# Feed-forward stages software-pipelined over batches, their square roots computed as powers on GpSimd

## The reference, cut to what matters

```python
def _ternary_linear(x, w):
    alpha = jnp.mean(jnp.abs(w))
    w_t = jnp.sign(w) * (jnp.abs(w) > 0.5 * alpha)          # weights -1, 0, 1
    rms = jnp.sqrt(jnp.sum(x * x, axis=-1, keepdims=True)) / jnp.sqrt(d)
    return jnp.einsum('bsd,fd->bsf', x / (rms + EPS), w_t)
h = gelu(_ternary_linear(_layernorm(x), w_up))              # 256 -> 1024
x = x + _ternary_linear(h, w_down)                          # 1024 -> 256
```

## Time and profile before

| | us |
|---|---|
| median of 3 runs (lowest, highest) | 3073.3 (3071.29, 3078.18) |
| the profiled execution, its own time | 3066.11 |
| its span in the profile | 3064.3 |
| busy: PE, DVE, ACT, POOL | 2203.0, 2319.1, 1555.3, 846.9 |
| feed-forward stage 1, from the first statistics to the last addition to x | 214.97 |
| feed-forward stage 2, likewise | 215.48 |

### The profile page before, as it was taken

One profiled execution on the slowest core, in us unless ns is written; L12 is line 12 of the kernel. 1 busy time (PEld: TensorE's weight loads), 2 busy tenths in 40 slices (PEclk: granted clock), 3 DMA queues, 4 the chain that ended last, 5 costly groups with the idle time before them and its releaser, 6 DMA issues. The chain is left out here.

```text
span 3064.3 us, 47620 instructions
## 1 busy us (share of the span) xinstructions
PE 2203.0 (72%) x12353; PEld 1739.3 (57%) x12353; DVE 2319.1 (76%) x5828; ACT 1555.3 (51%) x4161; POOL 846.9 (28%) x1482
## 2 busy tenths in 40 slices
PE   6777887776776877677777777778777775344676
PEld 3445555544444866666666666767666665333344
DVE  5555565556775099999999999999999999993566
ACT  3443344343664455555555555555555554443666
POOL 0000000000000055445544444444445444441000
PEclk7666556666887977777777767777777776655788
DMA  4000000000000000000000000000000000000000
GB/s 147 10 6 10 3 10 10 10 6 0 0 0 0 0 1 0 0 0 0 1 0 0 1 0 0 1 0 0 1 0 0 0 0 1 0 0 0 14 21 21
DMA packets 14136, 20.98 MB, mean 7 GB/s; under 512 B 1280, under 2 KB 12032, under 8 KB 13824
## 3 DMA queue, kind: packets, MB, share of 16 engines
q1 hardware_dynamic: 14080, 20.36, 2.2%
HBM read 12.27 MB, written 4.19 MB: 5 GB/s over the span
## 5 line engine op out<-in xcount | busy, mean ns | idle before, releaser
L554 PE MATMUL bank<-U,ident 128*128 128x128 f32 x2080 | 471.0, 398 | 121.2 <-ACT go L766 101.1
L1296 POOL TENSOR_TENSOR wu<-U,stg 128x256 f32<-128x256 f32 x512 | 318.6, 622 | 852.9 <-DVE U L1230 852.9
L554 PEld LDWEIGHTS bank<-U,ident 128*128 128x128 f32 x2080 | 434.6, 251 | 162.6 <-issue 71.9
L617 PE MATMUL bank<-stack,tm 128*128 128x64 f32 x1792 | 352.1, 386 | 218.6 <-ACT tm L703 218.6
L617 PEld LDWEIGHTS bank<-stack,tm 128*128 128x128 f32 x1792 | 340.8, 296 | 238.2 <-issue 238.2
L903 ACT ACTIVATE xs<-U 128x256 f32<-128x256 f32 x512 | 213.6, 417 | 468.4 <-DVE U L1230 466.3
L1180 DVE TENSOR_REDUCE pn<-xs 128x32 f32<-128x512 f32 x512 | 351.2, 686 | 29.4
L1249 POOL TENSOR_TENSOR stg<-R 128x128 f32 (+1 forms) x65 | 29.8, 459 | 1067.9 <-ACT stg L787 1067.9
L1253 POOL TENSOR_TENSOR kv<-stg 128x256 f32<-128x256 f32 x513 | 318.6, 621 | 1.6
L540 PE MATMUL bank<-wcat,yT 128*128 x1024 | 298.9, 452 | 3.0 <-issue 3.0
L675 ACT ACTIVATE prob<-bank,nmax 128x128 f32<-128x128 f32 x512 | 146.1, 368 | 240.1 <-DVE nmax L1024 239.3
(11 more groups left out here) (179 smaller groups left out, 4081.2 us busy)
## 6 DMA issues: line engine op xcount, KB each, us to landing
out_x<-x SPq DMA_DIRECT2D x8, 512.0 KB, 2.9
x<-in_x SPq DMA_DIRECT2D x1, 3584.0 KB, 16.3
Vs<-V SPq DMA_DIRECT2D x8, 272.0 KB, 3.4
lane<-in_lanes SPq DMA_DIRECT2D x8, 256.0 KB, 3.1
wcat<-in_wcat SPq DMA_DIRECT2D x1, 1792.0 KB, 13.0
Vs<-V SPq DMA_DIRECT2D x8, 204.0 KB, 2.7
wraw<-in_w_up SPq DMA_DIRECT2D x1, 1024.0 KB, 18.2
wraw<-in_w_down SPq DMA_DIRECT2D x1, 1024.0 KB, 10.9
```

What stands on the lines that cost most here:

```text
L554: last = pe.matmul(rsum.rearrange("p (t i) -> p t i", i=HD), ident[:, :], steps[:, :, :, j], start=(j == 0), stop=(j == HD - 1))
L617: last = pe.matmul(bank[3 + g][:, e * CH:(e + 1) * CH], tm[:, g * (PB // 2) + e, :, :].rearrange("p a c -> p (a c)"), stack[:, :], start=T ...
L1296: pool.tensor_tensor(ij(wu[:, :]), ij(U[:, half if j else 1 - half, (j - 1) % STEPS, :]), col(stg[:, half, j, TW, :]), ALU.mult).then_inc( ...
```

## The change

Edits, all within the feed-forward stages but for two constants:

1. Both roots go to POOL, in a new program part `ffn_pool`: `tensor_tensor` with the operation power and a tile of 0.5 (`halves`, one memset more on DVE at the start). Eight columns for the layer norm, four for the hidden rms. DVE now evacuates the sum of squares first (`s0`).
2. Applying the layer norm goes from DVE to ACT (`normalise`: Identity with scale and bias pointers), with one small DVE instruction more (`nbias`).
3. The next batch's rows, transposes and split move into the units: on DVE the statistics behind unit 0, the scale behind unit 1, the low parts behind unit 5; on ACT `normalise` behind units 1 and 2 (two tiles each), the high parts behind unit 4; on PE the transposes behind down of unit 3, and the next batch's up of unit 0 ahead of down of unit 7. `xh` gets a second buffer.
4. `recurrence_stats` goes from unit 5 to behind unit 6.
5. The column sums of `ssq` go to bank 4, beside the products.

```diff
+        halves = sb("halves", [P, 2 * NT])
+        nbias = sb("nbias", [P, NT], F32, early)
-        xh = sb("xh", [P, 2, KD, L], F16, mid)
+        xh = sb("xh", [P, 2, 2, KD, L], F16, mid)
...
         def ffn_pe(pe, i):
+            def transposes(q):
+                pe.wait_ge(F["xn"], q * NT + NT)
+                pe.wait_ge(F["lo"], q * KD)
...
+            transposes(i * (B + 1))
+            pe.wait_ge(F["hi"], i * (B + 1) * KD + KD)
+            pe.wait_ge(F["lo"], i * (B + 1) * KD + KD)
+            pe.wait_ge(F["g"], i * B * NF)
+            up(i * (B + 1) % 2, 0)
+            with pe.Fori(i * B, i * B + B) as b:
+                for n in range(NF):
+                    if n + 1 < NF:
+                        pe.wait_ge(F["g"], b * NF + n)
+                        up(par, n + 1)
+                    else:
+                        pe.wait_ge(F["hi"], q * KD + 2 * KD)
+                        pe.wait_ge(F["lo"], q * KD + 2 * KD)
+                        pe.wait_ge(F["g"], b * NF + n)
+                        up(par_next, 0)
+                    pe.wait_ge(F["hh"], b * NF + n + 1)
+                    pe.wait_ge(F["hl"], b * NF + n + 1)
+                    if n == 0:
+                        pe.wait_ge(F["x"], b * NT)
...
+                    if n == 3:
+                        transposes(pe.snap(b + (i + 1)))
                 pe.wait_ge(F["ss"], b * NF + NF)
                 for u in range(NT):
-                    last = pe.matmul(bank[0][:, u:u + 1], ssq[:, (NF - 1) % 2, u * P:(u + 1) * P], ones[:, 0:1],
+                    last = pe.matmul(bank[4][:, D + u:D + u + 1], ssq[:, (NF - 1) % 2, u * P:(u + 1) * P], ones[:, 0:1],
...
         def ffn_act(act, i):
-            act.activation(sd[:, :, :], vv[:, :, :], ACT.Sqrt).then_inc(F["sd"], 1)
+            def normalise(q, tile, u):
+                act.wait_ge(F["nb"], q + 1)
+                if u == 0:
+                    act.wait_ge(F["xt"], q * KD)
+                act.activation(xn[:, u, :], x[:, bass.ds(tile + u, 1), :].squeeze(1), ACT.Identity,
+                               bias=nbias[:, u:u + 1], scale=rstd[:, u:u + 1]).then_inc(F["xn"], 1)
...
-                act.activation(sd[:, :, :], vv[:, :, :], ACT.Sqrt).then_inc(F["sd"], 1)
-                act.wait_ge(F["sm"], b + 1)
-                act.activation(ysc[:, 0, :], bank[0][:, 0:NT], ACT.Sqrt, scale=1.0 / FF).then_inc(F["sr"], 1)
+                    if n in (1, 2):
+                        for u in range(2 * n - 2, 2 * n):
+                            normalise(q1, n1, u)
+                    if n == 4:
+                        act.wait_ge(F["up"], b * NF + i)
+                        for k in range(KD):
+                            split(q1, par_next, k)
+
+        def ffn_pool(pool, i):
+            def root(dst, src, e):
+                return pool.tensor_tensor(dst, src, halves[:, 0:e], ALU.pow)
...
+            with pool.Fori(i * B, i * B + B) as b:
+                pool.wait_ge(F["ve"], b * 2 + (2 * i + 4))
+                root(sd[:, :, :].rearrange("p a u -> p (a u)"), vv[:, :, :].rearrange("p a u -> p (a u)"), 2 * NT).then_inc(F["sd"], 1)
+                pool.wait_ge(F["s0"], b + 1)
+                root(ysc[:, 1, :], ysc[:, 0, :], NT).then_inc(F["sr"], 1)
...
             with dve.Fori(i * B, i * B + B) as b:
...
+                    if n == 0:
+                        layernorm_stats(q1, n1)
+                    if n == 1:
+                        layernorm_scale(q1)
+                    if n == 5:
+                        for k in range(KD):
+                            split(q1, par_next, k)
+                    if n == 6 and i == 0:
+                        recurrence_stats(dve, b, dve.snap((b + (B - 1)) % B * NT))
+                dve.wait_ge(F["sm"], b + 1)
+                dve.tensor_scalar(ysc[:, 0, :], bank[4][:, D:D + NT], 1.0 / FF, None, ALU.mult).then_inc(F["s0"], 1)
                 dve.wait_ge(F["sr"], b + 1)
-                dve.tensor_scalar(ysc[:, 1, :], ysc[:, 0, :], 1e-8, HI_H, ALU.add, ALU.mult).then_inc(F["s1"], 1)
+                dve.tensor_scalar(ysc[:, 2, :], ysc[:, 1, :], 1e-8, HI_H, ALU.add, ALU.mult).then_inc(F["s1"], 1)
```

More of the change, by code:

```diff
@@ L192, in build @@
         F = {n: sem("f_" + n) for n in (
-            "bs ag ve sd dn rs sc xn xt hi lo up g hh hl sq ss sm sr s1 s2 dnm x").split()}
+            "bs ag ve sd dn rs sc nb xn xt hi lo up g hh hl sq ss sm s0 sr s1 s2 dnm x").split()}
         C = {n: sem("c_" + n) for n in (
@@ L214, in ffn_pe @@
                     last.then_inc(F["xt"], 1)
[L215 to L222, removed]
-                        for part in range(2):
[L224 to L238, removed]
@@ new lines, in up @@
+            def up(par, n):
+                for part in range(2):
+                    for k in range(KD):
+                        last = pe.matmul(bank[2 + n % 2][:, :], wup[:, k, n * P:(n + 1) * P],
+                                         xh[:, bass.ds(par, 1), part, k, :].squeeze(1),
+                                         start=(part == 0 and k == 0), stop=(part == 1 and k == KD - 1))
+                last.then_inc(F["up"], 1)
+            pe.wait_ge(w_q, 2)
+            if i == 0:
+                pe.wait_ge(A["x2"], B * NT)
@@ new lines, in ffn_pe @@
+            transposes(i * (B + 1))
[4 more added lines that the diff above has]
+            with pe.Fori(i * B, i * B + B) as b:
+                q = pe.snap(b + i)
+                par = pe.snap((b + i) % 2)
+                par_next = pe.snap((b + (i + 1)) % 2)
+                for n in range(NF):
[11 more added lines that the diff above has]
+                        pe.wait_ge(F["x"], b * NT)
+                    for u in range(NT):
+                        for part in range(2):
+                            last = pe.matmul(bank[4 + u][:, 0:D], hh[:, n % 2, part, u * P:(u + 1) * P], wdn[:, n, :],
+                                             start=(n == 0 and part == 0), stop=(n == NF - 1 and part == 1))
+                    last.then_inc(F["dnm"], 1)
+                    if n == 3:
+                        transposes(pe.snap(b + (i + 1)))
@@ L245, in ffn_act, with split @@
         def ffn_act(act, i):
-            act.wait_ge(F["ve"], i * (B + 1) * 2 + 2)
-            act.activation(sd[:, :, :], vv[:, :, :], ACT.Sqrt).then_inc(F["sd"], 1)
+            def normalise(q, tile, u):
[4 more added lines that the diff above has]
+                               bias=nbias[:, u:u + 1], scale=rstd[:, u:u + 1]).then_inc(F["xn"], 1)
+            def split(q, par, k):
+                act.wait_ge(F["xt"], q * KD + k + 1)
+                act.activation(xh[:, bass.ds(par, 1), 0, k, :].squeeze(1), bank[k][:, :], ACT.Copy).then_inc(F["hi"], 1)
+            for u in range(NT):
+                normalise(i * (B + 1), 0, u)
+            for k in range(KD):
+                split(i * (B + 1), i * (B + 1) % 2, k)
             with act.Fori(i * B, i * B + B) as b:
[L249 to L252, removed]
+                q1 = act.snap(b + (i + 1))
+                par_next = act.snap((b + (i + 1)) % 2)
+                n1 = act.snap((b + 1) % B * NT)
                 for n in range(NF):
-                    act.wait_ge(F["up"], b * NF + n + 1)
+                    act.wait_ge(F["up"], b * NF + (n + 1 + i))
                     if n >= 2:
```

49 lines of the change are left out of this document (24 added, 25 removed).

## The result

| us | before | changed |
|---|---|---|
| median | 3072.3 (4 runs) | 3118.4 (4 runs, 3111.2 to 3122.7) |
| ratio, 95% interval | 1 | 1.0157 [1.0131, 1.0182] |
| profiled execution, its span | 3066.1, 3064.3 | 3122.7, 3120.9 |
| feed-forward stage 1, stage 2 | 214.97, 215.48 | 242.06, 232.70 |

The changed kernel is 1.6% slower, about 48 us. Forecast were 3080 and "slower"; 3118 lies in the range, but almost on the rival of the dear root (3115). The ratio gives 48 us, the two profiled spans 56.6. Of these 56.6 us, 44.3 lie in the two stages (27.1 and 17.2), 3.5 between them, and 8.7 ahead of stage 1. So I read the stages, not the span.

What follows compares the result with a forecast made beforehand. A chain from engine to engine was taken as the bound, no engine being full. Stage 1 +8.1, stage 2 −2.4 and a table load +1.3 made +7.0: 3080 us, range 3057 to 3135; the forecast's own case reached from +0 to +22.

Steps and rivals of the forecast that it cites:

- the rival of the dear root: POOL's root takes 1.5 us for four columns and 2.6 for eight: +35 more, about 3115; chance 0.27.
- steps 1 to 5: Last square to third Gelu: column sums and evacuation, POOL's root, additions, DVE's 5.15 us, two normalise tiles; 10.95 + R4.
- R4: POOL's power on four columns (hidden rms) at the batch boundary, without cover; taken as 0.7 us.
- 5.9 us less the normalisation: ACT's idle time before the third Gelu, beyond its table load (1.28) and two units (3.4).
- R8: POOL's power on eight columns (layer norm), taken as 1.1 us, covered for 1.2 by DVE's unit 1.
- my ends: Estimated limits of the power's price: 0.3 us for a few columns; at most 1.5 for four, 2.6 for eight.
- The clock: the rival that came in part: PE stays at 1.2 GHz beyond the boundary, one unit more at low clock: +20, about 3100; chance 0.09.
- The remainder: Third Gelu to a batch's last square: 12.4 us of ACT work and 1.0 of waits, 13.4.
- The recurrence statistics: Stage 1 only, on DVE behind unit 6: they delay unit 7's low part and sum, +1.5 per batch.
- The first batch of a stage: Cannot be overlapped: +1.6 before its first Gelu, +3.6 to the third, remainder +0.5, end −0.4; +5.3 per stage.
- The load behind stage 1: A Sqrt table load now ahead of the root of the 32 variances, with PE waiting behind: +1.3 us.
- the six units close up: Faster rival: R4 0.3, transposes cost no wait, recurrence statistics half hidden; −13, 3060; chance 0.16.

Runs made afterwards that it cites:

- the respaced kernel: low-first kernel with the next batch's statistics, scale, normalise, transposes and split each at least one unit apart, recurrence statistics behind unit 5; 3036.3 us, ratio 0.9877.
- the filled kernel: changed kernel with ten unread idle-filling matmuls on TensorE behind up of unit 1 and again behind up of unit 3; 3099.9 us, ratio 1.0097.
- low-first kernel: changed kernel with the next batch's rows spread further from the boundary and its unit 0 low part ahead of the batch-end waits and additions; 3074.9 us, ratio 1.0008.

## Why the prediction was right in sign, and where it was off

**What bounds the kernel: right.** A chain between engines, no full engine. From the changed kernel to the respaced one, over 80 us apart, DVE's and ACT's busy time in a stage differ by 1.2 us or less.

**Boundary, steps 1 to 5: right but for R4 and a wait.** With the measured 1.0 for R4, 10.95 + R4 gives 11.95; the wait for the eight-column root, 0.92, makes 12.9, and 12.9 was measured. Evacuation, additions, low part, statistics and scale were each where and as long as forecast, and `normalise` waited for `nbias`, with a gap of 6.9 instead of 5 to 6. (The "5.9 us less the normalisation" is a slip: 11.6 − 1.28 − 3.4 is 6.9, and 5.8 once the 1.1 is taken off.)

**R4 and R8: the step that failed.** I took 0.7 and 1.1 from the nearness to the cheap rows, with "the fixed 0.3 and 0.1 per column". Measured: 1.0 and 2.0. Of the 2.0, 1.64 are the power, and 0.37 stand there only where DVE's low part has started just before it; my sum had no term for that. From 1.01 and 1.64 I estimate 0.4 fixed and 0.16 per column: the form, a fixed part and a price per column, was right, and both of its numbers were too small. The cheap rows were no guide, since a product of four or eight columns takes 0.20. R8 then no longer fitted under its cover of 1.2. That is +0.3 and +0.9 per batch. Both values lay between my ends, well below the 1.5 and 2.6 of the rival; yet the time came out at the rival's 3115, because of the next points. That the two agree is chance.

**The clock: the rival that came in part.** It was priced at +20 as one long stretch, with 0.09. What came in stage 2 was a second fall: the wait for `nbias` also holds up down of unit 2, PE idles 3.35 us, and the next matmuls run at 1.2 GHz. The remainder, forecast 13.4, was 14.4; with the gaps filled it was 13.4. So the forecast of the remainder holds at 2.4 GHz, and the miss of 1.0 per batch in stage 2 is the clock. In stage 1 the filled kernel's period is 27.81, which is the forecast 26.5 with 0.3 + 0.9 for the power, to 0.1; the changed kernel's is 28.4 on average, so the clock costs 0.6 per period there.

**The recurrence statistics: right per batch, miscounted.** Behind unit 6 they cost 1.5, as forecast: 27.8 against 26.3 in the filled kernel. But I counted them in the seven periods only, and eight batches have them: the eighth's stand in the end of the stage, which is 7.3 us behind the last square instead of the forecast 5.4.

**The first batch of a stage.** Forecast +5.7 up to its last square; measured +9.4 and +9.1 (from the first statistics to the end of the last square 35.9 and 35.8 us instead of 26.5 and 26.7). Of stage 2's 3.4 too much, 0.4 stand before the first Gelu, 0.9 between it and the third (the wait for POOL), and 2.1 behind, where up and down run at the low clock again. Stage 1 has 3.7 too much.

**Sum.** Stage 2: forecast −2.4, measured +17.2. The excess of 19.6 is 7 × 1.3 for the power, 7 × 1.0 for the clock, 3.4 for the first batch and 0.4 for the end, to 0.3. Stage 1: forecast +8.1, measured +27.1; of the 19.0 too much, 7 × 1.3 are the power, 7 × 0.6 the clock, 3.7 the first batch and 1.9 the end, together 18.9. The load behind stage 1 was there as forecast: the root of the 32 variances starts 12.0 us behind the last addition instead of 10.7. The other 2.2 us between the stages I do not assign; that stretch differs between the profiled executions by more (1884.3 to 1892.6 us). POOL's first power took 1.64 us, so that nothing of the 6 us which the Trainium skill's GPSIMD Engine Reference (Instruction dispatch) gives for the first call of a freshly loaded kernel shows here.

**The chances.** Slower had 0.60, and was right, but for stage 2 the sign was wrong: it was forecast 2.4 us faster and is 17.2 slower. The forecast's own range ended at +22, 26 us short of the measured +48, because I priced the power and the clock as separate cases, while the wait for the first widens the gap behind which the second falls. The rival "the six units close up" was the right idea of what the pipelining could give, but needs another order than the change has: the respaced kernel shows it.

## What to carry to other kernels

When a step goes to another engine, write beside it in the plan when its operands are ready and when its result is read, in the reading engine's order: here a 2.0 us root had a cover of 1.2, and `normalise` none. Put statistics, root, scale, normalise, transposes and split of the next batch at least a unit apart, and ahead of a batch-end wait whatever is ready before it; these two turned +48 into −38 with nearly the same instructions in another order. Only then look at idle stretches of TensorE, since each can cost a second time through the clock.

## What I had not expected of the hardware

- GpSimd's power has a price per column: 1.01 us for four columns and 1.64 for eight, on 128 partitions, where a product takes 0.20 for either.
- Power and product of eight columns both last 0.37 us longer (2.01 and 0.57) when VectorE has started its low part (128x512) 0.17 us before. When the low part starts 0.09 us or more behind the power, nothing is added.
- The table load goes in front of the first activation of the loop, and takes that one's wait. Taking Sqrt out of the loop thus put a load on the path (+1.28 per batch) that had stood in idle time before; a small Gelu ahead of the wait moved it back.
- Two idle stretches of TensorE of about 3.4 us in a batch of 27 were each followed by a fall to 1.2 GHz in stage 2. The length of the idle stretch alone does not tell it: in stage 1, 3.04 and 3.27 us were not followed by one, and of two stretches of 2.72 us in the low-first kernel one was (a 1.91 behind it) and one was not (1.03). Ten matmuls in each gap that nobody reads, at 0.23 us each, kept the clock at 2.4 GHz in the batch shown and brought 18 us; eight in the respaced kernel likely 10.
